# Token part of a vision tower on one core: gate logits in column groups, attention operands side by side, gates stored by expert and token, output stores last in GpSimd's program

## The reference, cut to what matters

```python
h = _layernorm(h + attn(h))            # softmax(Q K^T / 8) V, 64 tokens per image, width 64
h = _layernorm(h + moe_top1(h))        # 8 experts, F = 256, softmax gate, capacity 1.25, nan_to_num
h = _layernorm(h + two_minGRU(h))      # two recurrent layers along the 64 tokens
h = _layernorm(h + _layernorm(h + moe_top2(h)) * gamma + beta)   # 16 experts, F = 128, best two gates
```

## Time and profile before

| | |
|---|---|
| median of 3 runs | 3005.96 us (2995.6 to 3011.03) |
| the profiled execution | 3004.41 us, of it the span in the trace 3002.6 us |
| busy: PE, PEld, DVE, ACT, POOL | 90%, 53%, 71%, 67%, 2% of the span |
| mean granted TensorE clock | 0.971 |
| spectral part and MLP | up to about 2554 us |
| token part | about 2554 to 2993 us, then the last store |

### The profile page before, as it was taken

One profiled execution on the slowest core, in us unless ns is written; L12 is line 12 of the kernel. 1 busy time (PEld: TensorE's weight loads), 2 busy tenths in 40 slices (PEclk: granted clock), 3 DMA queues, 4 the chain that ended last, 5 costly groups with the idle time before them and its releaser, 6 DMA issues.

```text
span 3002.6 us, 76054 instructions
## 1 busy us (share of the span) xinstructions
PE 2701.5 (90%) x28706; PEld 1597.0 (53%) x28706; DVE 2117.4 (71%) x4206; ACT 1997.2 (67%) x2415; POOL 69.5 (2%) x93
## 2 busy tenths in 40 slices
PE   5777789999898999898999888999999999999994
PEld 3444456666566666565666653444444443664441
DVE  6999777888676888776888755445444453677877
ACT  5888665777565777565777546778778787455551
POOL 0000000000000000000000002000000000100000
PEclk9999999999999999999999989999999999999996
DMA  3422255745455754364754343311111110114243
GB/s 104 125 108 106 88 187 167 230 179 179 142 179 161 234 180 179 134 199 157 231 186 174 141 153 81 82 50 60 50 47 49 50 60 0 30 30 102 54 86 63
DMA packets 160241, 361.59 MB, mean 120 GB/s; under 512 B 45878, under 2 KB 123734, under 8 KB 124246
## 3 DMA queue, kind: packets, MB, share of 16 engines
q1 hardware_dynamic: 136982, 185.95, 21.0%
q10 hardware_dynamic: 18432, 134.23, 11.0%
q0 software_dynamic: 4672, 39.20, 6.0%
HBM read 204.77 MB, written 154.53 MB: 120 GB/s over the span
## 4 chain that ended last, share of the span: by engine, by line
PE 74%; DVE 9%; issue 6%; ACT 6%; DMA 3%; SPq 1%; ACTq 0%; DVEq 0%; POOL 0%; POOLq 0%
PE pA L1514 16%; PE pA L1522 8%; PE pT L1609 8%; PE pS L1551 7%; PE pD L1598 5%; PE pD L1565 4%; PE pT L1540 4%; PE pD L1485 3%; PE pD L1580 3%; PE pA L1540 2%; DVE arena L1881 2%; ACT h_rows L1698 2%; PE pT L1619 2%; DMA h_scratch<-h_new 2%; PE pA L600 1%
## 5 line engine op out<-in xcount | busy, mean ns | idle before, releaser
L1848 DVE TENSOR_REDUCE small<-arena 128x32 f32<-128x1056 f32 x320 | 397.1, 1243 | 313.4 <-ACT arena L1683 306.5
L1514 PEld LDWEIGHTS pA<-conv_bd,h_in 128*128 128x128 f32 x4096 | 484.0, 194 | 96.1 <-issue 96.1
L1514 PE MATMUL pA<-conv_bd,h_in 128*128 128x128 f32 x4096 | 520.9, 281 | 1.9 <-DVE arena L1841 1.7
L1673 ACT COPY w_sb<-pA 128x1024 f32<-128x1024 f32 x256 | 259.4, 1013 | 254.0 <-PE pA L1522 236.2
L1694 ACT ACTIVATE h_new<-pT,bet,gam 128x1024 f32<-128x1024 f32 x256 | 307.1, 1200 | 153.2 <-PE pT L1540 136.2
L1862 DVE SCALAR_TENSOR_TENSOR w_sb<-w_sb,small 128x1024 f32<-128x1024 f32 x320 | 386.8, 1209 | 4.5 <-DVE h_new L1870 2.3
L1683 ACT ACTIVATE arena<-w_sb 128x1024 f32<-128x1024 f32 x320 | 338.9, 1059 | 10.2
L1551 PEld LDWEIGHTS pS<-cst,h_new 128*128 128x128 f32 x2048 | 221.4, 142 | 204.7 <-issue 133.5
L1540 PE MATMUL pT<-cst,w_sb 128*128 128x128 f32 x2048 | 279.1, 281 | 38.4 <-DVE w_sb L1862 20.4
L1551 PE MATMUL pS<-cst,h_new 128*128 128x128 f32 x2048 | 281.5, 281 | 24.8 <-ACT h_new L1694 22.2
L1540 PEld LDWEIGHTS pT<-cst,w_sb 128*128 128x128 f32 x2048 | 233.4, 144 | 103.5 <-DVE w_sb L1862 49.4
(11 more groups left out here) (316 smaller groups left out, 3489.7 us busy)
## 6 DMA issues: line engine op xcount, KB each, us to landing
h_scratch<-h_new ACTq DMA_DIRECT2D x128, 1024.0 KB, 4.4
h_in<-h_scratch SPq DMA_DIRECT2D x128, 1024.0 KB, 5.0
w_sb<-gates_scratch SPq DMA_DIRECT2D x168, 128.0 KB, 6.7
y_scratch<-w_sb POOLq DMA_DIRECT2D x32, 576.0 KB, 8.5
y_in<-y_scratch SPq DMA_DIRECT2D x512, 36.0 KB
w_sb<-in_L_tok_w1r_dram POOLq DMA_DIRECT2D x8, 576.0 KB, 6.8
w_sb<-in_L_tok_w1i_dram POOLq DMA_DIRECT2D x8, 576.0 KB, 6.7
w_sb<-in_L_tok_w2r_dram POOLq DMA_DIRECT2D x8, 576.0 KB, 7.0
```

The lines of the kernel that those rows point to most:

```text
L1514: pe.matmul(pA[:, c:c + 128], h_in[:, 1024 * n + c:1024 * n + c + 128], conv_bd[:], start=(j == 0), stop=False, skip_group_check=True)
L1848: dve.reduce_sum(var[n], sq[n % 2], axis=AX).then_inc(s["summed"], 1)
```

## The change

Gate logits: the gate weights become the stationary operand, padded to 32 columns (gwa, gwb), and the tokens stream; four groups of 256 tokens write partitions 0, 32, 64 and 96. This is a step of its own, gq1 or gq2. ScalarE copies the result (tile LG), and gl1 or gl2 is now two transposes of it into a "d" bank; VectorE adds the bias in `add_gate_bias`. Attention: Q and K of a tile's first 64 tokens go to partitions 0 to 63, those of its second 64 tokens to 64 to 127; V of even tiles to 0 to 63, of odd tiles to 64 to 127. So QT, KT, VB and PT are 128 x 512 instead of 64 x 1024, the scores use diagonal quadrants, pt is four full transposes, and pv fills two banks. Gates: VectorE writes them with the expert as the outer index (layer 1 in a tile of its own, gated1), the DRAM scratch is [expert, token], and a load is one row of 512 tokens. GpSimd stores all gates first and then the four output chunks. TOKEN_ORDER and the counts in TOKEN_SENDS are new. Lines cut here are the lists that name the new steps and the narrower loads of the gate weights.

```diff
 TOKEN_ORDER = """
-    xt1.0 qkv.0 xt1.1 sc.0 ex.0 qkv.1 pt.0 xt1.2 pv.0 qkv.2 xt1.3 xt2.0 sc.1 ex.1 sc.2 ex.2 gl1.0 pt.1 gx1.0 pt.2 cum.0 pv.1 qkv.3
-    gt1.0 e1.0 pv.2 e1.0 e1.0 xt2.1 e1.0 xt2.2 e1.0 e1.0 sc.3 gl1.1 e1.0 ex.3 gx1.1 e1.0 eb1.0 pt.3 wg.0 cum.1 gl1.2 yb1.0 pv.3
-    gt1.1 e1.1 e1.1 xt3.0 e1.1 gx1.2 gru0.0 xt2.3 e1.1 gru1.0 e1.1 gback.0 cum.2 e1.1 e1.1 xt4.0 gl1.3 gl2.0 gx2.0 gm2.0 e1.1
-    eb1.1 gt2.0 e2.0 e2.0 e2.0 e2.0 e2.0 e2.0 e2.0 yb1.1 e2.0 e2.0 gx1.3 e2.0 e2.0 xt3.1 e2.0 gru0.1 e2.0 cum.3 gru1.1 gt1.2 e2.0
-    e2.0 e2.0 gt1.3 e1.2 gback.1 e1.2 eb2.0 e1.2 e1.2 yb2.0 e1.2 e1.2 e1.2 e1.2 eb1.2 xt4.1 e1.3 e1.3 yb1.2 e1.3 e1.3 xt3.2 e1.3
-    gru0.2 gl2.1 e1.3 gru1.2 gx2.1 gm2.1 e1.3 gback.2 gt2.1 e1.3 e2.1 eb1.3 xt4.2 e2.1 e2.1 e2.1 yb1.3 e2.1 gl2.2 e2.1 e2.1 xt3.3
-    e2.1 gx2.2 gm2.2 e2.1 e2.1 gru0.3 e2.1 e2.1 e2.1 e2.1 gru1.3 gt2.2 e2.1 e2.1 gback.3 e2.2 e2.2 e2.2 e2.2 e2.2 eb2.1 xt4.3 e2.2
-    e2.2 gl2.3 e2.2 e2.2 e2.2 gx2.3 gm2.3 e2.2 e2.2 e2.2 e2.2 gt2.3 e2.2 e2.2 eb2.2 e2.3 yb2.1 e2.3 e2.3 e2.3 e2.3 e2.3 e2.3 yb2.2
-    e2.3 e2.3 e2.3 e2.3 e2.3 e2.3 e2.3 e2.3 e2.3 eb2.3 yb2.3
+    xt1.0 xt1.1 qkv.0 sc.0 ex.0 qkv.1 pt.0 pv.0 xt1.2 qkv.2 sc.1 xt2.0 sc.2 xt1.3 gq1.0 ex.1 ex.2 gl1.0 pt.1 gx1.0 wg.0 pt.2 cum.0
+    pv.1 qkv.3 gt1.0 e1.0 e1.0 sc.3 ex.3 pv.2 e1.0 pt.3 xt2.1 e1.0 e1.0 pv.3 gq1.1 e1.0 gl1.1 e1.0 e1.0 gx1.1 eb1.0 xt2.2 cum.1
+    xt2.3 yb1.0 gq1.2 gt1.1 e1.1 e1.1 xt3.0 e1.1 gru0.0 gl1.2 e1.1 gru1.0 e1.1 gback.0 e1.1 e1.1 xt4.0 gx1.2 cum.2 gq2.0 gq1.3
+    gl2.0 gx2.0 gm2.0 e1.1 gl1.3 eb1.1 gt1.2 gt2.0 e2.0 e2.0 e2.0 e2.0 gx1.3 yb1.1 e2.0 e2.0 e2.0 cum.3 e2.0 e2.0 xt3.1 e2.0
+    gru0.1 e2.0 e2.0 e2.0 e2.0 e2.0 e2.0 gru1.1 eb2.0 e1.2 yb2.0 e1.2 e1.2 e1.2 gback.1 e1.2 e1.2 e1.2 e1.2 eb1.2 gt1.3 xt4.1 e1.3
+    yb1.2 e1.3 gq2.1 e1.3 xt3.2 gl2.1 e1.3 gru0.2 e1.3 gru1.2 gx2.1 gm2.1 e1.3 gback.2 e1.3 gt2.1 e1.3 eb1.3 xt4.2 e2.1 e2.1 e2.1
+    gq2.2 yb1.3 gl2.2 e2.1 e2.1 e2.1 xt3.3 gx2.2 e2.1 e2.1 gru0.3 e2.1 e2.1 e2.1 e2.1 gm2.2 gru1.3 e2.1 e2.1 e2.1 gback.3 gt2.2
+    e2.1 e2.2 e2.2 e2.2 e2.2 e2.2 e2.2 e2.2 xt4.3 e2.2 gq2.3 eb2.1 e2.2 gl2.3 e2.2 e2.2 gx2.3 gm2.3 yb2.1 gt2.3 e2.2 e2.2 e2.2
+    e2.2 e2.2 e2.3 e2.3 e2.3 eb2.2 e2.3 e2.3 e2.3 e2.3 yb2.2 e2.3 e2.3 e2.3 e2.3 e2.3 e2.3 e2.3 e2.3 e2.3 eb2.3 yb2.3
 """
-TOKEN_SENDS = dict(xt1=(0, 2), qkv=(4, 2), sc=(1, 0), pt=(0, 2), pv=(1, 0), xt2=(2, 0), xt4=(2, 0), gl1=(1, 0), gl2=(1, 0), cum=(1, 0),
+TOKEN_SENDS = dict(xt1=(0, 2), qkv=(2, 1), sc=(1, 0), pt=(0, 1), pv=(2, 0), xt2=(2, 0), xt4=(2, 0), gq1=(0, 1), gq2=(0, 1), gl1=(1, 0), gl2=(1, 0), cum=(1, 0),
...
-        gwa, gwb = param(P, E1), param(P, E2)
+        gwa, gwb = param(P, 32), param(P, 32)
-        QT, KT, VB, PT = ([arena[0:64, 2048 * i + 1024 * j:2048 * i + 1024 * j + 1024] for j in range(2)] for i in range(4))
+        QT, KT, VB, PT = ([arena[:, 1024 * i + 512 * j:1024 * i + 512 * j + 512] for j in range(2)] for i in range(4))
         gates1, gates2 = arena[:, 8192:8192 + E1 * NT], arena[:, 8448:8448 + E2 * NT]
+        gated1 = arena[:, 8960:8960 + E1 * NT]
+        LG = [y_in[:, 512:768], cst[:, 128:384]]
-        g1_dram = nc.dram_tensor("gates1_scratch", [NCH, CT * E1, P], F32, kind="Internal").ap()
-        g2_dram = nc.dram_tensor("gates2_scratch", [NCH, CT * E2, P], F32, kind="Internal").ap()
+        g1_dram = nc.dram_tensor("gates1_scratch", [NCH, E1, CT * P], F32, kind="Internal").ap()
+        g2_dram = nc.dram_tensor("gates2_scratch", [NCH, E2, CT * P], F32, kind="Internal").ap()
...
-                for j in range(2):
-                    for which, w in (("d", wq), ("s", wk)):
-                        b = bank(which)
-                        sent(which, pe.matmul(b[0:64, :], w, XT[:, 1024 * c + 512 * j:1024 * c + 512 * j + 512], start=True, stop=True))
-                for j in range(2):
-                    b = bank("d")
-                    for i in range(8):
-                        a = 1024 * c + 512 * j + S * i
-                        mm = pe.matmul(b[0:64, S * i:S * i + S], XT[:, a:a + S], wv, start=True, stop=True)
-                    sent("d", mm)
+                for which, w in (("d", wq), ("s", wk)):
+                    b = bank(which)
+                    x = XT[:, 1024 * c:1024 * c + 1024].rearrange("p (t h q) -> p h t q", h=2, q=S)
+                    for h in range(2):
+                        mm = pe.matmul(b[64 * h:64 * h + 64, :].rearrange("p (t q) -> p t q", q=S), w, x[:, h], start=True, stop=True)
+                    sent(which, mm)
+                b = bank("d")
+                for m in range(4):
+                    for h in range(2):
+                        for u in range(2):
+                            a = 1024 * c + 256 * m + 128 * u + 64 * h
+                            q = 128 * m + 64 * h
+                            mm = pe.matmul(b[64 * u:64 * u + 64, q:q + 64], XT[:, a:a + S], wv, start=True, stop=True)
+                sent("d", mm)
...
-                        a = 128 * i + 64 * h
-                        mm = pe.matmul(b[64 * h:64 * h + 64, S * i:S * i + S], QT[c % 2][:, a:a + 64], KT[c % 2][:, a:a + 64], start=True, stop=True)
+                        q, a = slice(64 * h, 64 * h + 64), slice(S * i, S * i + S)
+                        mm = pe.matmul(b[q, a], QT[c % 2][q, a], KT[c % 2][q, a], start=True, stop=True)
-                for j in range(2):
-                    b = bank("s")
-                    for i in range(4):
-                        t = CT * c + 4 * j + i
-                        mm = pe.transpose(b[0:64, 128 * i:128 * i + 128], Sx[:, S * t:S * t + S], ident)
-                    sent("s", mm)
+                b = bank("s")
+                for m in range(4):
+                    mm = pe.transpose(b[:, 128 * m:128 * m + 128], chunk(Sx, c)[:, 128 * m:128 * m + 128], ident)
+                sent("s", mm)
-                b = bank("d")
-                for i in range(CT):
-                    for h in range(2):
-                        a = 128 * i + 64 * h
-                        mm = pe.matmul(b[64 * h:64 * h + 64, S * i:S * i + S], PT[c % 2][:, a:a + 64], VB[c % 2][:, a:a + 64], start=True, stop=True)
-                sent("d", mm)
+                for u in range(2):
+                    b = bank("d")
+                    rows = slice(64 * u, 64 * u + 64)
+                    for m in range(4):
+                        for h in range(2):
+                            a = 128 * m + 64 * h
+                            mm = pe.matmul(b[64 * h:64 * h + 64, S * m:S * m + S], PT[c % 2][rows, a:a + 64], VB[c % 2][rows, a:a + 64], start=True, stop=True)
+                    sent("d", mm)
...
-            def logits(E, gw, split):
 
                 def step(c):
                     taken("d", split, c)
+                    b = bank("s")
+                    for j in range(4):
+                        a = 1024 * c + 256 * j
+                        mm = pe.matmul(b[32 * j:32 * j + 32, 0:256], gw, XT_split[:, a:a + 256], start=True, stop=True)
+                    sent("s", mm)
+                return step
+
+            def turn_logits(layer):
+
+                def step(c):
+                    taken("s", f"gq{layer}", c)
                     b = bank("d")
-                    for i in range(CT):
-                        t = CT * c + i
-                        mm = pe.matmul(b[:, E * i:E * i + E], XT_split[:, 128 * t:128 * t + 128], gw, start=True, stop=True)
+                    for i in range(2):
+                        mm = pe.transpose(b[:, 128 * i:128 * i + 128], LG[layer - 1][:, 128 * i:128 * i + 128], ident)
                     sent("d", mm)
...
-                      gt1=turn_gates(E1, gates1, "gated"), gt2=turn_gates(E2, gates2, "pair_gated"),
+                      gt1=turn_gates(E1, gated1, "gated"), gt2=turn_gates(E2, gates2, "pair_gated"),
...
-                for j in range(2):
-                    act.copy(KT[c % 2][:, 512 * j:512 * j + 512], take()[0:64, :]).then_inc(s["ts_free"], 1)
+                act.copy(KT[c % 2], take()[:]).then_inc(s["ts_free"], 1)
-                for j in range(2):
-                    act.copy(PT[c % 2][:, 512 * j:512 * j + 512], take()[0:64, :]).then_inc(s["ts_free"], 1)
+                act.copy(PT[c % 2], take()[:]).then_inc(s["ts_free"], 1)
+            def keep_logits(layer):
+
+                def step(c):
+                    act.copy(LG[layer - 1], take()[:, 0:256]).then_inc(s["ts_free"], 1)
+                return step
...
+            by_expert = lambda a, w: a.rearrange("p (e t) -> p t e", e=w)
-                for j in range(2):
-                    dve.tensor_copy(QT[c % 2][:, 512 * j:512 * j + 512], take()[0:64, :]).then_inc(s["td_free"], 1)
-                for j in range(2):
-                    dve.tensor_copy(VB[c % 2][:, 512 * j:512 * j + 512], take()[0:64, :]).then_inc(s["td_free"], 1)
+                dve.tensor_copy(QT[c % 2], take()[:]).then_inc(s["td_free"], 1)
+                dve.tensor_copy(VB[c % 2], take()[:]).then_inc(s["td_free"], 1)
```

(37 more changed lines are left out.)

9 lines of the change are left out of this document (5 added, 4 removed).

## The result

| | median | range | runs |
|---|---|---|---|
| before, in this comparison | 3000.78 us | 2992.24 to 3011.03 | 4 |
| after | 2961.59 us | 2953.67 to 2965.36 | 4 |

The ratio is 0.9866, interval 0.9831 to 0.9901. The profiled execution took 2959.79 us, span 2958.0.

A forecast was written before the change was run, and what follows sets the result against it. Token part taken as paced by TensorE in stretches, by VectorE at the end, broken by waits for gate rows from DRAM. Terms 8.5 + 3 + 3 + 1 + 5 + 6.4, about 27 us, gave 2979 us; range 2962 to 3001.

The forecast's parts named there:

- The start: Token part up to gt1.0: side-by-side attention matmuls, fewer copies and transposes save 8.5 us, ends -4 and -10.
- The logits: Gate logits in column groups: about 1.2 us of TensorE saved a step, helping the -3 us up to gt2.0.
- Rival 1: Attention pairs and logit column groups don't overlap as older forms do: about -14 us, 2992 us, chance 0.15.
- The gate loads: Gate reads from DRAM: longer pieces cut landing from 6.48 to 4.5 us, saving 2 us a round trip.
- The stage up to gt1.2: From gt2.0 to gt1.2: -3 us, ends 0 and -5, capped by TensorE's loss of 5.7 us.
- The stage up to gt2.3: From gt2.1 to gt2.3: -5 of TensorE's 7.6 us lost there, ends -2 and -8.
- Two signs: VectorE: no gate wait above 1 us after 2830; if the sum is wrong, its waits on TensorE grow instead.
- The order: Token part: moved steps cover gate round trips, including gt2.1's 3.19 us; just-in-time gt1.3 costs 0 to +3 us.
- The tail's -6.4: Last stretch: yb2.1 moved ahead of gt2.3's use covers that round trip, -6.4 us, ends -4 and -7.
- The stores: Output stores moved behind gt2.3 in GpSimd's order: gain 0; without cover their traffic would cost up to 2 us.
- Rival 2: Gate loads: piece length worth nothing, landing stays 6.48 us, just-in-time places bite; about -14 us, 2992 us, chance 0.17.
- Rival 3: Layer 2's experts: gate loads get slower and DMA paces the stage, +29 us, 3035 us, chance 0.06.

The follow-up runs named there:

- c_before: The kernel before run once more, nothing changed: token part 450.9 us, ratio 1.0006.
- all_but_o: The changed kernel with the old order of steps, each gq a step or so ahead of its gl: token part 420.0 us, ratio 0.9900.
- odd_pitch: The kernel before with one empty 512-byte row after each tile's gate rows in the scratch: token part 429.2 us, ratio 0.9931.
- al: The kernel before with the new attention operands and column-grouped gate logits only, old layout and order: token part 440.7 us, ratio 0.9970.
- g_512: The kernel before with gates stored by expert, scratch padded so loads are 512-byte pieces 1 KB apart: token part 429.1 us, ratio 0.9924.
- g_4k: The kernel before with gates stored by expert, loads in 512-byte pieces 4 KB apart in both layers: token part 467.8 us, ratio 1.0080.
- g_only: The kernel before with gates stored by expert and token alone, one 2 KB row a partition per load: token part 432.3 us, ratio 0.9944.

## Why the prediction was right or wrong

The order of steps differs between before and after, so stages can be compared only between kernels of the old order. These are the times between the first records of the gate turns in TensorE's timeline (c_before: 44.0, 147.8, 191.2, 269.0, 364.9 after the first transpose), which cut the token part almost where the prediction's sum does:

| stage, in the trace of before | forecast, all parts | all_but_o | odd_pitch | al |
|---|---|---|---|---|
| start to gt1.0 (2598.7) | -8.5 | -6.6 | +0.1 | -9.6 |
| to gt2.0 (2700.8) | -3 | -3.8 | 0.0 | -3.1 |
| to gt1.2 (2744.1) | -3 | -7.6 | -7.6 | +1.5 |
| to gt2.1 (2822.4) | -1 | +0.7 | -0.1 | +0.5 |
| to gt2.3 (2916.0) | -5 | -9.0 | -9.2 | -1.0 |
| to the end (3002.6) | -6.4 | -4.6 | -4.9 | +1.5 |
| sum | -26.9 | -30.9 | -21.7 | -10.2 |

A minus is time saved against c_before. In sum the last two columns add up to the first within 1 us; in the first row they don't, by 2.9 us, which is all_but_o's longer dip. Against the trace of before in place of c_before the sums are -28.0, -18.7 and -7.3, and the stage to gt2.3 is 6.7 and 6.9 us shorter in all_but_o and odd_pitch.

**The start: right. The logits: right in price, not shown in the time.** 8.5 us were forecast for the start; attention and logits together took 9.6 off the time to gt1.0 (44.0 to 34.4, at clocks of 0.96 and 0.95; those are the times of c_before and al). The attention alone took 8.5 off the token part, and 6.6 off the time to gt1.0 in a profile whose start ran at 0.86. L500's successor takes 1.87 us for eight records, as worked out. The logits' 0.68 us were taken as 0.5, the copy's 0.38 as 0.4. But their -3 up to gt2.0 isn't shown to be theirs: that stage is 3.7 us shorter with the attention alone, 3.3 with the logits alone and 3.1 with both. gt1.0 was expected near 2590, which is 35 us after the start; it stands at 33.9. Rival 1 fell with the rows of the chain.

**The gate loads: the step that failed.** "I take 4.5", between 6.48 and 3.0, "nearer the broad load in piece length". The landing is 3.0 us, my lower bound; the reason I gave for a value above it, a repeated read, costs nothing that shows, and the reason for the gain, piece length, is wrong (g_512). The mechanism was another: the pitch. With 4.5 us three stages (to gt1.2, to gt2.3 and to the end) were to give 3 + 5 + 6.4 = 14.4 us with the order's and the logits' help; the layout alone gave 7.6 + 9.2 + 4.9 = 21.7. The stage up to gt1.2 went past its bound of -5, since I had capped it at TensorE's loss of 5.7 us. Windows of that stage, before and then odd_pitch:

```profile
2700.80:2744.10 43.30, 37.60 (x157) 17.43 (x155) 31.30 (x58) 23.19 (x37) 0.57 (x1) 0.96 0.53 101
```

```profile
2701.40:2737.20 35.80, 35.80 (x158) 16.37 (x156) 30.03 (x55) 22.88 (x37) 0.59 (x1) 1.00 0.43 122
```

TensorE's idle time fell from 5.7 us to nothing, the whole of the cap, and its busy time fell by 1.8 us besides, for the same work: the clock rose from 0.96 to 1.00. (c_before had 0.96 too, g_512 and all_but_o 1.00.) The forecast had put this at nothing. The stage up to gt2.3 went past its -8 only against c_before, whose clock averaged 0.95 there; against the trace of before it stayed inside. The wait of a first expert is only the part of a late load that shows as one: VectorE's waits fell by 27.4 us between c_before and g_512 (32.5 to 5.1), the token part by 21.8: most of the waiting was on the path, and I had counted about half of it there. Two signs that I had named came out as forecast: no wait on gates after 2830 (the last, 2.13 us, ends at 2759.54), and VectorE's waits on TensorE didn't grow by what the gates' waits lost. Summed over the token part they fell, from 30.7 to 24.4 us.

**The order: wrong cause.** The tail's -6.4 was credited to yb2.1 in front of gt2.3's use. The layout alone gives 4.9 of it, in the old order; with the order and without the stores a wait of 7.23 us stands there. Behind gt1.0 the order is worth 1.0 us beside all the other edits and 2.6 beside the layout. The sum of 27 was missing some 7 us: along 449.5, 440.7, 420.0 and 415.5 it is 8.8 for attention and logits, 20.7 for the layout and 4.5 for the order, together 34; some 3 of the last belong to the dip in all_but_o's start, and so to the layout.

**The stores: right in the whole, wrong in the reason.** Priced at 0, measured 0 (413.7 against 413.6 and 417.4). But the cost without cover, "up to 2 us" of crossing traffic, missed the mechanism: in the new order a store left at yb2.1 stands ahead of gt2.3's in GpSimd's program, and beside slow loads that costs some 8 us (456.0 and 447.6, one profile each). I had looked only for what stood ahead in the old order.

**Rival 2 was half right.** Piece length is worth nothing, as it said. It then let the loads stay at 6.48 us, because it, too, had only the length as a cause. **Rival 3** had slower loads as a danger of the new layout; g_4k is the kernel that it describes, by another mechanism, 18 us slower in the token part.

**The range.** Its far ends summed to 38 us off, 2968 on the median of 3005.96, and 4 were taken off for the clock. The true change is about 34 us on the token part, inside those ends. What took the time past the edge by 0.4 us was the basis: in this comparison the kernel before had a median of 3000.78, 5.2 below the one that I had counted from. By the second ratio the time would be 0.9894 x 3000.78 = 2969. On which side of 2962 it fell was luck; that the layout's term was too small wasn't.

## What to carry to other kernels

Before a landing time is put down to the size of the pieces, write down the addresses: which offsets the pieces of one DMA have, and which those of the DMAs in flight beside it, and whether they agree modulo 2, 4 or 8 KB. A row of padding tells it apart in one run, and was worth as much here as the whole new layout (odd_pitch 0.9931, g_only 0.9944). Split a DMA's median by stage before it is used as a term: 4.7 and 7.9 us stood side by side in the trace of before, and a median of 6.7 hid them. A part that measures nothing in the finished kernel may have been needed on the way there: test it also beside the old version of what covers it (the stores' place, 8 us by single profiles beside loads of 6.8 us, 0 beside 3.0). And before two profiles are taken apart stage by stage, compare the granted clock of each stage: 3 us of what looked like the order's worth was one dip.

## What the runs showed of the hardware

- A 128 KB load of four 512-byte pieces a partition, each row read by 64 partitions, lands in 3.1 us at a pitch of 1 KB, 4.5 at 2 KB, 5.0 at 4 KB with the experts skewed, 11.7 at 4 KB without, 7.9 at 8 KB with the experts skewed (second layer of before), and 3.2 at 4.5 and 8.5 KB. At 1 and 2 KB the experts weren't skewed.
- With pieces of 1 KB at a pitch of 2 KB it lands in 3.1 us, as whole rows of 2 KB do in 3.0.
- Runs of one and the same kernel spread from 2987.67 us (granted clock 0.976) to 3017.14 (0.969). A stretch at the lower level that is longer in one profile than in the other moves the token part by 3 us (0.96 and 0.89 over the start of g_512 and g_only).
- Where TensorE idled 5.7 of 43.3 us for late gates, its granted clock averaged 0.96 over the stage; where it idled none, 1.00, and the same work took 1.8 us less busy time (before and odd_pitch).
